# Attention operands turned by transposing DMA transfers instead of TensorE, in a vision-transformer layer kernel

## The reference

```python
h = einsum("bpk,ek->bpe", patches, W) + b              # 256 tokens x 256 features
q, k, v = layernorm(h) @ wq, @ wk, @ wv                # 16, 4, 4 heads of 16
q, k = rope(q), rope(k)
attn = softmax(where(causal, q @ k.T / 4, -inf))       # each k head serves 4 q heads
h = h + (attn @ v) @ wo
h = h + ffn(layernorm(h))                              # one scale over all images, so it comes last
```

## Time and profile before

| | before |
|---|---|
| median of the runs | 961.52 us |
| the profiled execution's own time | 966.27 us |
| its span in the trace | 964.5 us |
| mean granted TensorE clock | 0.962 of full speed |
| busy: PE / DVE / ACT / POOL | 86% / 76% / 66% / 54% |
| DMA moved | 50.41 MB, mean 52 GB/s |

### The profile page before, as it was taken

One profiled execution on the slowest core, in us unless ns is written; L12 is line 12 of the kernel. 1 busy time (PEld: TensorE's weight loads), 2 busy tenths in 40 slices (PEclk: granted clock), 3 DMA queues, 4 the chain that ended last, 5 costly groups with the idle time before them and its releaser, 6 DMA issues.

```text
span 964.5 us, 26048 instructions
## 1 busy us (share of the span) xinstructions
PE 831.7 (86%) x9061; PEld 490.0 (51%) x9070; DVE 735.9 (76%) x1309; ACT 632.9 (66%) x988; POOL 519.8 (54%) x545
## 2 busy tenths in 40 slices
PE   3788999999999999999999999999998859997775
PEld 2445555555555555555555555555554434443443
DVE  5845777777777777777777777777776659999898
ACT  3246666666666766666666666766766549996664
POOL 1345666566556656666666656556654327774000
PEclk8679999999999999999999999999999779999899
DMA  7000111111111111111111111111100000001488
GB/s 264 29 1 2 39 41 41 54 52 47 38 38 38 38 38 38 38 38 38 38 38 38 51 47 55 38 38 38 39 13 12 13 22 1 0 0 41 143 262 251
DMA packets 33158, 50.41 MB, mean 52 GB/s; under 512 B 2016, under 2 KB 28384, under 8 KB 33120
## 3 DMA queue, kind: packets, MB, share of 16 engines
q1 hardware_dynamic: 33120, 49.91, 16.4%
HBM read 33.13 MB, written 16.78 MB: 52 GB/s over the span
## 4 chain that ended last, share of the span: by engine, by line
PE 55%; DVE 26%; issue 10%; ACT 4%; POOL 1%; DVEq 1%; DMA 1%; ACTq 0%; SPq 0%; POOLq 0%
PE pair L439 10%; DVE act_all L1240 9%; PE pair L464 7%; PE pair L510 6%; PE pair L517 5%; PE pair L548 5%; PE pair L583 5%; PE pair L729 4%; DVE act_all L1281 4%; PE pair L494 3%; PE pair L532 3%; PE pair L552 2%; ACT ffn L986 2%; PE pair L572 2%; DVE ffn L1504 2%
## 5 line engine op out<-in xcount | busy, mean ns | idle before, releaser
L1240 DVE TENSOR_REDUCE act_all<-pair 128x8 f32<-128x1024 f32 x192 | 235.2, 1225 | 101.8 <-PE pair L517 101.1
L869 ACT ACTIVATE act_all<-pair 128x768 f32<-128x768 f32 x256 | 207.9, 812 | 135.0 <-PE pair L534 135.0
L1030 POOL TENSOR_SCALAR_AFFINE_SELECT act_all<-act_all 128x512 f32<-128x512 f32 x256 | 162.7, 641 | 101.9 <-ACT act_all L869 101.9
L1073 POOL TENSOR_TENSOR act_all<-act_all 128x2 f32<-128x2 f32 x64 | 60.9, 951 | 213.9 <-DVE act_all L1273 143.4
L439 PE MATMUL pair<-act_all 128*128 128x256 f16 (+1 forms) x960 | 120.7, 281 | 9.3 <-DVE act_all L1175 9.3
L861 ACT ACTIVATE act_all<-pair 128x1024 f16<-128x1024 f16 x64 | 65.7, 1027 | 79.2 <-PE pair L494 79.2
L439 PEld LDWEIGHTS pair<-act_all 128*128 128x128 f16 (+1 forms) x960 | 92.6, 100 | 28.1 <-issue 15.7
L510 PE MATMUL pair<-act_all,eye_b 128*128 128x512 bf16 x256 | 79.2, 392 | 26.5 <-DVE act_all L1240 25.9
L548 PE MATMUL pair<-act_all 128*32 128x256 f32 x1024 | 83.6, 399 | 1.3 <-POOL act_all L1030 1.2
L1068 POOL TENSOR_TENSOR act_all<-act_all 128x1280 f16<-128x1280 f32 x31 | 80.9, 2611 | 1.3 <-ACT act_all L799 1.3
L517 PEld LDWEIGHTS pair<-act_all 32*128 32x128 f16 x1536 | 43.9, 94 | 68.2 <-issue 66.9
(11 more groups left out here) (136 smaller groups left out, 1685.2 us busy)
## 6 DMA issues: line engine op xcount, KB each, us to landing
act_all<-x_t SPq DMA_DIRECT2D x32, 640.0 KB, 4.0
out<-act_all SPq DMA_DIRECT2D x32, 256.0 KB, 2.2
ffn<-out SPq DMA_DIRECT2D x16, 512.0 KB, 4.7
out<-ffn SPq DMA_DIRECT2D x16, 512.0 KB, 3.2
act_all<-w_down SPq DMA_DIRECT2D x1, 704.0 KB, 8.7
act_all<-w_emb SPq DMA_DIRECT2D x1, 640.0 KB, 3.9
ffn<-w_gate SPq DMA_DIRECT2D x1, 640.0 KB, 7.0
ffn<-w_up SPq DMA_DIRECT2D x1, 640.0 KB, 7.8
```

What stands on the lines that cost most here:

```text
L869: act.activation(probs[:, o:o + 2, 0:3, :].rearrange("p h k s -> p h (k s)"), pair[1][:, :].rearrange("p (h c) -> p h c", h=2)[:, :, 0:3 * P],
L1030: pool.affine_select(out=p, in_=p, pattern=[[0, 4], [1, P]], compare_op=ALU.is_ge, fill=0.0, base=0, channel_multiplier=-1).then_inc(maske ...
L1240: dve.tensor_reduce(to.rearrange("p (g k) -> p k g", g=GROUPS)[:, first:first + 2, :], pair[2][:, :].rearrange("p (k g t) -> p k g t", k=2 ...
```

## The change

- `max_turn`, `stack_turn`, `max_turned` and `stacked` go, with their 30 transposes and 5 copies an image. SP issues transposing DMA transfers in their place: `turn_max` one transfer of `max_stack` (128 x 1280 in 2-byte elements, 320 KB) to `max_op`; `turn_stack` four transfers of `stack` (together 128 x 2560, 640 KB) to `qk_op`, which holds keys and queries of an image: first two for queries 4 to 7 and the keys ("upper", 2 x 192 KB), then two for queries 0 to 3 ("lower", 2 x 128 KB).
- `stack` becomes two buffers. `score_pair` takes the upper queries in its first four pairs; `o_copy` swaps its two halves accordingly.
- SP's loop is written out for all steps: in each it loads an image, stores a result, issues `turn_stack` of image n+1 and then `turn_max` of image n+2.
- `JOBS` shrinks from twelve to eight places; both token blocks of the patch product go into one bank and are read by one `embedded` of 512 columns.

```diff
-JOBS = [("patch", 0), ("patch", 1), ("max_t", 0), ("max_t", 1), ("o_t", 0), ("o_t", 1), ("x_t", 0),
-        ("stack_t", 0), ("qkv", 0), ("qkv", 1), ("on_t", 0), ("out", 0)]
+JOBS = [("patch", 0), ("o_t", 0), ("o_t", 1), ("x_t", 0), ("qkv", 0), ("qkv", 1), ("on_t", 0), ("out", 0)]
...
+            def turn_max(n):
+                sp.wait_ge(high_ready, n * 2 + 2)
+                sp.wait_ge(low_ready, n + 1)
+                if n > 0:
+                    sp.wait_ge(unit_scored, n * PAIRS_U)
+                sp.dma_start_transpose(max_op.rearrange("p b g t -> p (b g) t"),
+                                       max_stack.rearrange("p b h k -> p (b h k)")).then_inc(max_turned[n % 2], 16)
+            def turn_stack(n):
+                sp.wait_ge(stack_copied, n * 2 + 2)
+                sp.wait_ge(stack_high, n + 1)
+                sp.wait_ge(max_ready, n + 1)
+                if n >= 2:
+                    sp.wait_ge(scored, (n - 1) * PAIRS_S)
+                for first, last, turned in ((4, 10, upper_turned), (0, 4, lower_turned)):
+                    for tb in range(TB):
+                        sp.dma_start_transpose(
+                            qk_op[n % 2][:, first:last, tb * P:(tb + 1) * P],
+                            stacks[n % 2][:, tb, 2 * first:2 * last, :].rearrange("p h k -> p (h k)")
+                        ).then_inc(turned[n % 2], 16)
+            next_x(2)
+            for n in range(-2, IMAGES + 1):
+                if n + 5 < IMAGES:
+                    next_x(n + 5)
+                if n >= 1:
+                    store_h1(n - 1, (n - 1) % 2)
+                if 0 <= n + 1 < IMAGES:
+                    turn_stack(n + 1)
+                if n + 2 < IMAGES:
+                    turn_max(n + 2)
...
                 if p == 0:
-                    pe.wait_ge(read["max_t"], y.n * 2 + 1)
-                    wait(pe, read["stack_t"], y.n * 3)
-                if p == 2:
-                    pe.wait_ge(read["max_t"], y.n * 2 + 2)
+                    pe.wait_ge(max_turned[y.parity], y.half * 16 + 16)
...
                 if i == 0:
-                    pe.wait_ge(read["stack_t"], x.n * 3 + 2)
+                    pe.wait_ge(upper_turned[x.parity], x.half * 32 + 32)
                 if i == PAIRS_S // 2:
-                    pe.wait_ge(read["stack_t"], x.n * 3 + 3)
+                    pe.wait_ge(lower_turned[x.parity], x.half * 32 + 32)
...
-            def embedded(x, tb):
+            def embedded(x):
                 z = x + 2
-                act.wait_ge(done["patch"], z.n * 2 + (tb + 1))
+                act.wait_ge(done["patch"], z.n + 1)
```

More of the change, by code:

```diff
@@ L362, in _, with next_x @@
             sp.dma_start(down_n, w_down.rearrange("(c p) i -> p c i", p=P)).then_inc(ffn_loaded, 16)
-            for n in (2, 3):
+            def next_x(n):
                 sp.wait_ge(x_high_ready, n - 1)
@@ L413, in take_bank @@
                 at = JOBS.index(job)
-                back = 2
-                while True:
+                for back in range(1, 4 * len(JOBS)):
                     turn, place = divmod(at - back, len(JOBS))
@@ L428, in patch @@
                 z = x + 2
-                b = take_bank(x, ("patch", tb))
+                b = shared[JOBS.index(("patch", 0)) % 2][:, tb * D:(tb + 1) * D]
+                if tb == 0:
+                    take_bank(x, ("patch", 0))
                 if x.known and z.n == 0 and tb == 0:
@@ L438, in patch @@
                     for sx, sw in PARTS:
-                        mm = pe.matmul(b[:, 0:D], xs[0:k, sx, c, tb * P:(tb + 1) * P], we[0:k, sw, c, :],
+                        mm = pe.matmul(b, xs[0:k, sx, c, tb * P:(tb + 1) * P], we[0:k, sw, c, :],
                                        start=(c == 0 and (sx, sw) == PARTS[0]),
                                        stop=(c == KC - 1 and (sx, sw) == PARTS[-1]))
-                mm.then_inc(done["patch"], 1)
+                if tb == TB - 1:
+                    mm.then_inc(done["patch"], 1)
             def x_turn(x):
@@ L797, in x_high @@
                 act.wait_ge(xt_loaded[v.parity], v.half * 16 + 16)
-                wait(act, done["patch"], v.n * 2 - 2)
+                wait(act, done["patch"], v.n - 1)
                 act.activation(x_parts[v.parity][:, 0], xt[v.parity], ACT.Copy).then_inc(x_high_ready, 1)
@@ L829, in high @@
                 act.wait_ge(qk_ready, z.n + 1)
-                wait(act, done["max_t"], z.n * 2)
+                wait(act, max_turned[z.parity - 1], (z + -1).half * 16 + 16)
                 wait(act, stack_copied, z.n * 2)
@@ L1221, in fill_stack @@
                 dve.wait_ge(low_ready, y.n + 1)
-                wait(dve, done["stack_t"], y.n * 3)
+                wait(dve, upper_turned[y.parity], y.half * 32)
+                wait(dve, lower_turned[y.parity], y.half * 32)
+                stack = stacks[y.parity]
                 dve.tensor_copy(stack[:, :, :, 0:32], max_stack).then_inc(stack_copied, 1)
@@ L1225, in fill_stack @@
                                   max_stack[:, :, HEADS:QK, 0:16], ALU.subtract).then_inc(stack_copied, 1)
-            def max_turned(x):
-                y = x + 1
-                dve.wait_ge(done["max_t"], y.n * 2 + 1)
-                wait(dve, unit_scored, y.n * PAIRS_U)
-                dve.tensor_copy(max_op[:, :, 0:P],
-                                shared[JOBS.index(("max_t", 0)) % 2][:, 0:320].bitcast(FP16).rearrange(
-                                    "p (g t) -> p g t", g=5)).then_inc(read["max_t"], 1)
             def reduce_pair(x, p):
@@ L1257, in norm_stats @@
                 z = x + 2
-                dve.wait_ge(read["patch"], z.n * 2 + 2)
+                dve.wait_ge(read["patch"], z.n + 1)
                 fence(dve)
```

118 lines of the change are left out of this document (25 added, 93 removed).

## The result

The changed kernel took 1143.06 us (median of 4 runs, 1140.85 to 1145.77) where the kernel before took 961.5: a ratio of 1.188 [1.185, 1.192]. The profiled execution took 1145.77 us, span 1143.7. The direction was right, the size was not: +181.5 us where +76.5 was forecast.

What follows compares the result with a forecast made beforehand. TensorE was taken as nearly the bound, with a chain in the step's first half. 30 steps of +2.3 (+69) and ends (+8) gave 966.3 + 77 = 1043, 1038 us as median against 961.5; range 975 to 1095, with rivals 945 to 1180.

Steps and rivals of the forecast that it cites:

- The maximum operand lands late and sets the step: First unit pair on TensorE must start by T + 7.0 but waits for this operand; each microsecond later lengthens the step one.
- T + 9.9: Forecast landing of the maximum operand, T + 2.6 + x; T is the start of a step's first patch matmul.
- +2.3 us a step: Forecast step change: (2.6 + x) - 7.0 - 0.63 at x = 7.3; 30 steps, +69 us.
- x = 7.3 us: Time for 960 KB as transposing transfers: geometric middle of 4.5 (by bytes) and 11.7 (by pieces).
- the four issues ahead of it take about 0.4 us each as the plain ones do: SP's four stack issues before the maximum operand's were priced like plain issues, ending at T + 2.8.
- The rate of 261 GB/s: Skill page's effective bandwidth of transposing DMA; by it x would be 3.8 us, the case of rival 1.
- rival 3: TensorE's clock falls after each wait, some 3.5 us of matmuls at 1.2 GHz: +1.7 us a step, about 1090; chance 0.12.
- What is removed is worth 0.63 us a step: First-half chain: eight transposes 0.46 plus VectorE's copy L1231 0.39, less 0.22 for the wider `embedded` read.
- The ends: First turning step and last two, where nothing covers the transfers: about 4 us against 1.5 to 2, together +8.
- Rival 1: Transfers at plain rate, x = 4.5, operand at T + 7.1, step -0.5 us, 951 in all; chance 0.28.
- Rival 2: Pieces at full packet price, x = 11.7, operand at T + 14.3, step +6.7 us, 1176 in all; chance 0.15.
- Rival 4: The 30 128x128 blocks do not overlap, 1.4 us each, step 46 us, about 1700 in all; chance 0.03.

Runs made afterwards that it cites:

- fill_10_5: The changed kernel with 5 filler matmuls before score pair 0's wait and 10 before the first unit pair's; 1047.84 us, 1.090.
- plain_late: The kernel before, transposes on TensorE, its first unit pair made to wait for a chain of three plain 320 KB transfers; 1112.5 us, 1.154.
- order_max: The changed kernel with the maximum operand's transfer issued between upper and lower stack, and `low` written right behind the maxima; 1011.03 us, 1.050.
- max_only: The kernel before with only the maximum operand turned by DMA, the stack still on TensorE; 960.74 us, 1.000.
- one_stack: The changed kernel with one 640 KB transposing transfer for the whole stack in place of four; 1057.9 us, 1.098.
- two_stack: The changed kernel with the stack laid out by head pair, upper (384 KB) and lower (256 KB) one transfer each; 1036.07 us, 1.080.
- best_d: best_b with VectorE's `fill_stack` moved from behind its second reduction to behind its first; 958.9 us, 0.9964 to the kernel before.
- best_a: two_stack's layout with order_max's order, `fill_stack` moved behind the second reduction, `o_turn` 0 ahead of score pair 0, no fillers; 1021.33 us, 1.060.
- best_b: best_a plus filler matmuls, one ahead of score pair 0 and four ahead of score pair 1; 1104.5 us, 1.147.

## Why the prediction was right or wrong

- **The maximum operand lands late and sets the step: right.** Forecast T + 9.9, measured T + 9.91; upper operand forecast T + 5.5, and TensorE goes on at T + 5.42 (537.76). TensorE waits for it at L505 and for the upper operand at L528. The +2.3 us a step are the +2.2 that fill_10_5 shows with the clock held, and that kernel's 1048 us lies by the forecast 1038.
- **Its working: right only in the sum.** I put the issues at 0.4 us each, from the plain store, and made up for it with x = 7.3 us for the bytes, the middle of two bounds. In fact four issues take 5.2 us, and the bytes pass at 213 KB per us, the lower bound. From the first issue to the last landing it is 8.7 us either way. This is chance, and it hid what mattered: a price per issue points to fewer transfers as well as to another order, one per byte only to another order. The place where the term went wrong is the step "the four issues ahead of it take about 0.4 us each as the plain ones do".
- **The rate of 261 GB/s.** By this figure of the Trainium skill (DMA: Bandwidth & Descriptors, Latency and other measured facts) 983 KB would have taken 3.8 us, an estimate. The trace agrees in part: while the engines work they move 207 to 227 GB/s here, not far below that; over the whole 8.7 us it is 113 GB/s, because they rest between SP's issues. For this series the rate alone was no guide.
- **The rest of the step at full clock: wrong, and this is what failed.** The prediction took the whole of +2.3 us at the level of rows 1 and set the clock apart as rival 3, at 0.12, with "some 3.5 us of matmuls" and +1.7 us a step. The clock is at 0.50 for 12 of 29 us in the step shown, and at 0.80 in the mean of the pipeline's middle; it costs 3.5 us a step, twice that. The reason to think it unlikely, "the wait would be a single one", was wrong twice. One long wait is enough: in plain_late one of 2.88 us costs 1.6 us a step in clock, about the 1.7 of rival 3. And it isn't single: there are three waits in the step (1.07, 0.98, 2.37 us). The first follows from the prediction's own figures (upper operand wanted at T + 4.3, landing at T + 5.5). The second stands where the transposes that I priced at nothing had been: they were worth nothing as time, but they kept TensorE at work in that hole, and filling these two waits gave order_max 42 us. The row that I had from the first steps (L439 in 3.16 us, clock 0.72 over 40 us) came with waits of 1.33 us, shorter than the 2.5 that I forecast for every step; it should have made this the likeliest case. With 3.5 for 1.7 the sum is 1038 + 107 = 1145 us, against 1143 measured; that it fits this closely is partly luck, as the ends below show.
- **What is removed is worth 0.63 us a step: too much.** L1231 gave 0.14 of its 0.39 us (max_only). The 0.46 of the transposes ahead of the second patch product were not measured alone. The forecast of +2.3 doesn't hang on it, since what VectorE saves moves the time at which the operand is wanted by as much.
- **The ends: mis-sized, in both directions.** +8 forecast. In fill_10_5's profile the whole is 84.5 us more than before, of which 31 x 2.23 = 69 are the steps; 15 are ends. In after's the whole is 179.2 us more and 31 x 5.69 = 176 are steps, so 3 are ends: the last steps cost less than a full step's lateness and clock.
- **Rival 1 (in time, faster)** did not come about: the transfers run at the rate of plain ones, as it said, but its T + 7.1 needed the issues to be free. **Rival 2** gave nearly the measured time (1176) by a mechanism that isn't there: the operand lands at 9.9, not at 14.3. **Rival 4** was far off.
- **The second half**, said to stay at 11.2 us, is 14.05 (547.36 to 561.41). The added 2.85 us are clock, since fill_10_5 has 11.2 us there again: that condition of failure did occur.

## What to carry to other kernels

Price a new wait on TensorE twice, once for the wait and once for the matmuls behind it at half the clock, and count as waits the holes that open where covering work is taken out. Where the profile of before shows such waits anywhere, even in its first steps, its clock there is the row to take. On a queue in order ask what a transfer stands behind and what each issue takes; here another order (with `low` written earlier) was worth 132 us in the changed kernel and two issues for four 107, but the latter only 11 once the order was right and the clock held. And when a step of VectorE is moved, look at what GpSimd does at the new time.

## What the runs showed of the hardware

- The issue of a transposing transfer keeps SP busy: mostly 1.2 to 1.4 us for 128 to 320 KB, 1.44 for 384 KB and 2.9 to 3.1 for 640 KB (one_stack), against 0.34 and 0.40 for the plain loads of 640 KB and stores of 256 KB in the pipeline. Size isn't all: directly behind a transfer of 384 KB, one of 256 KB takes 1.65 us (two_stack) and one of 320 KB too (best_d). From the start of the issue to the landing the median is 2.7 us for 128 to 192 KB and 3.4 for 320 KB (after), and 5.0 for 640 KB (one_stack).
- 15 more matmuls of 512 columns a step made the kernel 95 us faster, and eight more took order_max from 1011 to 969. Waits of 0.34 and 0.99 us in a step (best_a) were followed by some 7 us at 0.50 of the clock in each step; the three waits of 0.44 to 0.52 us in a step of before were not, nor were the waits of 0.99 and 1.24 us that fill_10_5 keeps. In two_stack nearly the same three waits (0.7, 1.0 and 0.7 us) were followed by full clock in one step and by ten microseconds of low clock in the next.
- VectorE and GpSimd: two fp16 copies of 128x640 take 0.55 us while GpSimd is idle (best_d) and 3.13 beside its TENSOR_TENSOR of 128x1280 (best_b). Two subtractions of 128x64 take 0.35 us, and 1.68 beside its two TENSOR_TENSOR of 128x320 (best_b).
- A copy of 0.47 us between BATCH_NORM_STATS2 and BATCH_NORM_AGGREGATE costs 0.14 to 0.16 us.
